# Audio tower on one core: expert pairs spread over row 7's attention, biases on VectorE, row 5's route earlier

## What is computed

```python
h = _L0_tok_ref(x, ...)      # per row: gelu(x W1 + b1), gelu(. W2 + b2), . W3 -> sigmoid -> lengths;
                             # Xnew = interp_weights(cumsum(lengths)) @ x      (750 -> 375 tokens)
h = h + _L0_attn_ref(_layernorm(h), ...)
                             # rmsnorm, qkv; softmax(q) over the 64 of a head, softmax(k) over tokens + 8 memory
                             # keys; context = k v^T; out = context q; @ w_out + b_out; rmsnorm
h = h + _L0_ffn_ref(_layernorm(h), ...)
# in _L0_ffn_ref, over all rows together:
routes = jnp.argmax(probs, axis=-1)
pos = jnp.take_along_axis(jnp.cumsum(oh, axis=0), routes[:, None], axis=1)[:, 0] - 1
y = jnp.einsum('ecd,efd->ecf', buf, expert_w) + expert_b[:, None, :]
out = jnp.where(keep[:, None], gathered, xf) * route_probs[:, None]
```

## Time and profile before

| what | value |
|---|---|
| median of 3 runs | 478.9 us (478.19 to 482.76) |
| the profiled execution, its own time | 480.63 us |
| its span in the trace | 478.8 us |
| mean granted TensorE clock in it | 0.953 |
| TensorE, VectorE, ScalarE, GpSimd busy | 421.4, 361.0, 190.6, 136.2 us |
| start of step 7's values of row 6, end of its layer 2 | 348.5, 362.4 us |
| the ending (after layer 2 of row 7) | 362.4 us to the end of the span |

### The profile page before, as it was taken

The page is one execution under the profiler, slowest core; times in us unless marked ns, Lnnn a source line. Parts: engine busy times, 40 slices in busy tenths (PEclk is TensorE's granted clock), DMA queues, the critical chain, the costliest instruction groups (busy, mean ns, idle before and its releaser), DMA issues.

```text
span 478.8 us, 7541 instructions
## 1 busy us (share of the span) xinstructions
PE 421.4 (88%) x2535; PEld 363.6 (76%) x2535; DVE 361.0 (75%) x946; ACT 190.6 (40%) x377; POOL 136.2 (28%) x189
## 2 busy tenths in 40 slices
PE   3976699999999999999999999999996869987790
PEld 2755587898889788978897988789886847776790
DVE  3543867896999799979988998899899456438761
ACT  2412414831582177128604841593154227520000
POOL 4200120013026313530451055007304410004682
PEclk9997899999999999999999999999999979998885
DMA  5674002000100100020002000200000361130133
GB/s 168 155 269 133 1 2 64 2 0 24 43 2 18 43 23 1 18 64 2 2 18 64 2 1 17 65 1 13 6 1 0 80 104 42 41 84 11 31 94 94
DMA packets 30795, 21.57 MB, mean 45 GB/s; under 512 B 4666, under 2 KB 28312, under 8 KB 30390
## 3 DMA queue, kind: packets, MB, share of 16 engines
q1 hardware_dynamic: 27862, 18.73, 13.8%
q0 software_dynamic: 2880, 2.35, 2.1%
q10 hardware_dynamic: 16, 0.02, 0.0%
HBM read 14.41 MB, written 6.62 MB: 44 GB/s over the span
## 4 chain that ended last, share of the span: by engine, by line
PE 59%; DVE 14%; issue 12%; SPq 5%; DMA 4%; POOL 3%; ACT 2%; POOLq 0%; ACTq 0%; DVEq 0%
PE psB L875 7%; PE psB L877 7%; PE psB L876 7%; PE psC L901 6%; PE psC L838 4%; PE psC L1002 4%; PE psC L839 4%; PE psC L840 4%; DMA xt<-in_x 3%; DVE qsum L1403 2%; POOL A L575 2%; PE psC L985 2%; SPq L407 2%; DVE rs L1362 2%; DVE h2b L1293 1%
## 5 line engine op out<-in xcount | busy, mean ns | idle before, releaser
L875 PE MATMUL psB<-W2h,h1l 128*125 128x512 f32 x192 | 79.0, 412 | 0.0
L877 PE MATMUL psB<-W2h,h1h 128*125 128x512 f32 x192 | 77.0, 401 | 0.0
L876 PE MATMUL psB<-W2l,h1h 128*125 128x512 f32 x192 | 76.8, 400 | 0.0
L619 ACT ACTIVATE h2b<-h2b 125x512 f32<-125x512 f32 x48 | 30.3, 631 | 99.7 <-DVE h2b L1286 99.6
L1286 DVE TENSOR_TENSOR h2b<-psB,b2r 125x512 f32<-125x512 f32 x48 | 33.0, 688 | 20.8 <-PE psB L877 20.3
L877 PEld LDWEIGHTS psB<-W2h,h1h 128*125 128x125 f32 x192 | 36.4, 190 | 9.1
L493 POOL TENSOR_TENSOR sg<-euler,sg 125x6 f32<-125x6 f32 x8 | 15.2, 1896 | 98.0 <-DVE sg L1300 98.0
L876 PEld LDWEIGHTS psB<-W2l,h1h 128*125 128x125 f32 x192 | 36.7, 191 | 7.9
L875 PEld LDWEIGHTS psB<-W2h,h1l 128*125 128x125 f32 x192 | 36.6, 191 | 8.0 <-DVE h1l L1277 0.2
L614 ACT ACTIVATE h<-psA,b1c 128x376 f32<-128x376 f32 x64 | 36.0, 580 | 15.2 <-PE psA L840 14.9
L1293 DVE CUSTOM_DVE_ANT_0 h2b<-h2b,W3r 125x512 f32<-125x512 f32 x48 | 32.3, 684 | 2.8 <-ACT h2b L619 2.7
(11 more groups left out here) (248 smaller groups left out, 1004.2 us busy)
## 6 DMA issues: line engine op xcount, KB each, us to landing
xt<-in_x SPq DMA_DIRECT2D x8, 375.0 KB
xs<-in_x SPq DMA_DIRECT2D x8, 312.5 KB
slot_x<-ebr SPq DMA_DIRECT2D x2, 960.0 KB, 9.2
basef<-in_L_tok_W SPq DMA_DIRECT2D x1, 1024.0 KB, 6.1
ebr<-in_L_ffn_expert_b SPq DMA_DIRECT2D x1, 1024.0 KB, 6.8
ewf<-slot_x SPq DMA_DIRECT2D x2, 480.0 KB, 6.3
h2b<-slot_x SPq DMA_DIRECT2D x2, 480.0 KB, 8.1
slot_y<-h SPq DMA_DIRECT2D x4, 240.0 KB, 2.5
```

The costliest lines, as they stand in the source:

```text
L619: nc.scalar.activation(slot, slot, ACT.Gelu).then_inc(c_g2.sem, 1)
L875: mm(ps, lo, W2h[:, k, :], start=k == 0, stop=False)
L876: mm(ps, hi, W2l[:, k, :], start=False, stop=False)
L877: last = mm(ps, hi, W2h[:, k, :], start=False, stop=k == HK - 1)
```

## The change

- Step 7 only: TensorE does row 5's `xf_transposed` between row 6's values and queries, its `logits` behind the queries and its `positions` behind group 4 of layer 2, and then row 6's keys. VectorE does `normal2`, `take_logits`, `route` and `place_in_expert` of row 5 between row 6's query maxima. Row 6's first keys wait for `place_in_expert` of row 5 (c_pp), and positions wait for c_xl instead of c_ke.
- The ending: the expert pairs begin right behind row 6's attend and stand between all of row 7's steps. Row 6's xf, logits and positions stand around row 7's attend.
- The bias matmul is gone. `expert_bias(p)` on VectorE adds the bias while it moves psB to ya and yb; ScalarE's `take_outputs` is gone, and one semaphore, s_eyb, takes the place of s_ya and s_yb.
- `take_m` of row 6 moves from VectorE to ScalarE (four scaled copies). Row 7's moments1 and normal1 go ahead of row 6's out_norm on VectorE; row 6's moments2 and normal2 come later.
- GpSimd does the scatter of row 5 ahead of row 7's sigmoid power, and the first three fetches around row 7's norm2 and norm3.
- The dense experts: 6, then 4 of row 6's, then row 7's 16, then row 6's last 6. Row 6's choice is spread in xn instead of osq. Rows finish in the order 0, 1, 7, 2, 6, 3, 4, 5.

The diff, cut to its core:

```diff
-        ROW_ORDER = [0, PRIOR, 1, 2, 3, LAST, 4, 5]
+        ROW_ORDER = [0, 1, LAST, 2, PRIOR, 3, 4, 5]
...
             def ending():
+                scatter(PRIOR - 1, PRIOR - 2)
                 sigmoid_pow(LAST, PRIOR)
-                scatter(PRIOR - 1, PRIOR - 2)
                 norm1(LAST, PRIOR)
                 norm2(PRIOR, PRIOR - 1)
                 norm3(PRIOR, PRIOR - 1)
                 counts(PRIOR, PRIOR - 1)
-                norm2(LAST, PRIOR)
-                norm3(LAST, PRIOR)
                 after(pool, c_idx, SLOT_ROWS - 1, 9)
                 pool.wait_ge(s_yst, 128)
                 fetch(0)
+                norm2(LAST, PRIOR)
+                fetch(1)
+                norm3(LAST, PRIOR)
+                fetch(2)
                 counts(LAST, PRIOR)
-                for b in range(1, SLOT_ROWS):
+                for b in range(3, SLOT_ROWS):
...
+            def take_m(b, prev):
+
+                after(act, c_m, b, 1)
+                after(act, c_rk, b, 1)
+                if prev is not None:
+                    after(act, c_fin, prev, 1)
+                for p in range(PAIRS):
+                    last = nc.scalar.activation(m[:, p, :], psC[1][:, p * C:(p + 1) * C], ACT.Copy, scale=rk[:, p:p + 1])
+                last.then_inc(c_ms.sem, 1)
...
+                if row_is(b, PRIOR) and p == 0:
+                    after(pe, c_pp, b - 1, 1)
...
-                if f is not None:
+                if row_is(f, PRIOR):
+                    after(pe, c_xl, f, 1)
+                elif f is not None:
                     after(pe, c_ke, f, 1)
...
             def expert_products(p):
                 pe.wait_ge(s_exc, p + 1)
-                if p == 0:
-                    pe.wait_ge(s_eb, 16)
                 if p < 2:
                     after(pe, c_b2, LAST, TJ)
                 else:
-                    pe.wait_ge(s_ya, p - 1)
-                    pe.wait_ge(s_yb, p - 1)
+                    pe.wait_ge(s_eyb, p - 1)
                 ps, xT = psB[p % 2], sxT[:, p % 2, :]
-                bias = ebr[0:1, 2 * p:2 * p + 2, :].rearrange("p e c -> p (e c)").unsqueeze(1).to_broadcast([1, 2, 2 * C])
-                mm(ps[0:TS, :].rearrange("p (t n) -> p t n", t=2), ones[0:1, 0:TS], bias, start=True, stop=False)
                 for i in range(2):
                     w = ewT[:, 2 * p + i, :]
...
                 last.then_inc(s_ey, 1)
...
                 if f is not None:
                     for j in range(GJ):
                         values(f, before(f), j)
+                if m == LAST:
+                    xf_transposed(k, m)
+                if f is not None:
                     for j in range(GJ):
                         queries(f, before(f), j)
+                if m == LAST:
+                    logits(k, m)
                 if m is not None:
                     layer2(m, before(m), 4)
-                if k is not None:
+                if m == LAST:
+                    positions(k, f)
+                if k is not None and m != LAST:
                     xf_transposed(k, m)
                 if f is not None:
                     keys(f, before(f), 0)
-                if k is not None:
+                if k is not None and m != LAST:
                     logits(k, m)
                 if f is not None:
                     for p in range(1, PAIRS):
...
                 if m is not None:
                     x_next(m, k)
                     layer2(m, before(m), 5)
-                if k is not None:
+                if k is not None and m != LAST:
                     positions(k, f)
...
                 warp(f, before(f))
                 fold(k, before(k))
                 attend(k, before(k))
+                expert_tokens(0)
                 xn_transposed(f, before(f))
+                expert_tokens(1)
+                expert_products(0)
                 for j in range(GJ):
                     values(f, before(f), j)
-                queries(f, before(f), 0)
-                expert_tokens(0)
-                queries(f, before(f), 1)
-                queries(f, before(f), 2)
+                expert_tokens(2)
+                for j in range(GJ):
+                    queries(f, before(f), j)
+                expert_products(1)
                 keys(f, before(f), 0)
-                expert_products(0)
-                expert_tokens(1)
+                expert_tokens(3)
+                expert_products(2)
                 keys(f, before(f), 1)
-                expert_products(1)
-                expert_tokens(2)
+                expert_tokens(4)
+                expert_products(3)
                 keys(f, before(f), 2)
+                expert_tokens(5)
+                expert_products(4)
                 keys(f, before(f), 3)
-                expert_products(2)
-                expert_tokens(3)
+                expert_tokens(6)
+                expert_products(5)
                 for j in range(KJ):
                     k_transposed(f, k, j)
-                expert_products(3)
-                expert_tokens(4)
+                expert_tokens(7)
+                expert_products(6)
+                context(f, k)
+                expert_products(7)
+                for j in range(GJ):
+                    q_transposed(f, k, j)
+                fold(f, k)
                 xf_transposed(k, None)
-                context(f, k)
-                expert_products(4)
-                expert_tokens(5)
+                attend(f, k)
                 logits(k, None)
-                for j in range(GJ):
-                    q_transposed(f, k, j)
-                expert_products(5)
-                expert_tokens(6)
-                fold(f, k)
                 positions(k, None)
-                expert_products(6)
-                expert_tokens(7)
-                expert_products(7)
-                attend(f, k)
                 chosen_on_rows(k)
                 dense_bias(k)
-                for e in range(9):
+                for e in range(6):
                     dense(k, e)
                 xf_transposed(f, None)
                 logits(f, None)
-                for e in range(9, E):
+                for e in range(6, 10):
                     dense(k, e)
                 chosen_on_rows(f)
                 positions(f, None)
                 dense_bias(f)
                 for e in range(E):
                     dense(f, e)
+                for e in range(10, E):
+                    dense(k, e)
...
+            def expert_bias(p):
+                if p == 0:
+                    dve.wait_ge(s_eb, 16)
+                    after(dve, c_h1l, LAST, 2)
+                    after(dve, c_warp, LAST, 1)
+                dve.wait_ge(s_ey, p + 1)
+                pair = slice(2 * p, 2 * p + 2)
+                ps = psB[p % 2][:].rearrange("p (e c) -> p e c", c=C)
+                vec.tensor_tensor(ya[:, pair, :], ps[0:TS, 0:2, :], ebr[0:TS, pair, :], ALU.add)
+                vec.tensor_tensor(yb[:, pair, :], ps[0:TS, 2:4, :], ebr[0:TS, pair, :], ALU.add).then_inc(s_eyb, 1)
...
+                if m == LAST:
+                    normal2(k, before(k))
                 if f is not None:
                     query_max(f, before(f), 0)
-                if k is not None:
+                if k is not None and m != LAST:
                     normal2(k, before(k))
+                if m == LAST:
+                    take_logits(k, before(k))
+                    route(k, before(k))
                 if f is not None:
                     query_max(f, before(f), 1)
                     query_max(f, before(f), 2)
+                if m == LAST:
+                    place_in_expert(k, before(k))
                 if m is not None:
...
-                take_m(k, r)
                 moments1(f, k)
+                normal1(f, k)
                 out_norm(k, r)
-                normal1(f, k)
+                xn_lo(f, k)
                 residual(k, r)
-                xn_lo(f, k)
-                moments2(k, r)
-                for j in range(GJ):
-                    query_max(f, k, j)
-                for p in range(PAIRS):
-                    key_max(f, k, p)
-                normal2(k, r)
                 keep_h(f, k)
+                expert_bias(0)
+                query_max(f, k, 0)
+                query_max(f, k, 1)
+                expert_bias(1)
+                query_max(f, k, 2)
+                expert_bias(2)
+                key_max(f, k, 0)
+                key_max(f, k, 1)
+                expert_bias(3)
+                key_max(f, k, 2)
+                key_max(f, k, 3)
+                expert_bias(4)
                 key_sum(f, k)
+                expert_bias(5)
                 query_sum(f, k)
                 query_norm(f, k)
+                expert_bias(6)
+                moments2(k, r)
+                expert_bias(7)
+                normal2(k, r)
+                take_m(f, k)
                 take_logits(k, r)
                 route(k, r)
                 spread_choice(k)
+                out_norm(f, k)
```

(32 more changed lines are left out.)

70 lines of the change are left out of this document (26 added, 44 removed).

## The result

The changed kernel takes 482.96 us (median of 9 runs), the kernel before 478.9. The ratio is 1.008, interval 1.0049 to 1.0111: 0.4 to 1.1% slower. The 0.8% lies within the 1% that I called no change, but it goes the other way than my forecast, and the time is 1 us above my range. The profiled execution took 482.93 us with a span of 481.1.

A forecast was written before the change was run, and what follows sets the result against it. TensorE was busiest, but row 7's chain through GpSimd's order set the end. 467.6 for the experts + 3.4 finishes + 3.8 store gave span 474.8, a 4.0 us gain; 475.0 us predicted, range 467.5 to 482.

The forecast's parts named there:

- Part 1: Step 7, row 5's route ahead of row 6's queries: layer 2's group 5 +6.3 us, row 6's attend +7.3 us.
- +7.3 for +7.95: Row 7's power starts 7.95 us later; VectorE used to take it 0.4 late, so row 6's attend moves 7.3.
- Parts 2 and 3: Biases to VectorE (8.4 us off TensorE) and pairs between row 7's steps: attend(7) carried at 420.4, 8.7 us early.
- Part 4: GpSimd's and VectorE's order behind attend(7): most gain given back, row 7's first token at 449.6, was 451.12.
- dense 9, chosen and positions 1.2: Behind row 7's logits, after route and four row 6 tokens: ninth expert, chosen and positions add 1.2 us.
- 8.7 us shrink to 1.5: Of attend(7)'s 8.7 us lead, 1.5 us is left at row 7's first token.
- Part 5: Last stretch: 22 experts end at 467.6, four finishes take 3.4, the store 3.8; span 474.8, a 4.0 us gain.
- then the store, 3.8: At the end: 3.8 us from the last finish to the end of the span, for the store.
- the upper half-rate choice: Last 22 experts: half rate for up to 6.9 us, upper end of 16.9 to 18.7 us.
- the detour's number (480.0): Rival: step 7's route costs over 6.3 us, with group 4, keys and group 5 at half; no difference, chance 0.16.
- The slow one: Rival: the last stretch's 22 experts stay at half rate, 487.2 us, chance 0.10.
- The quicker one: Rival: clock stays up after short gaps and the scatter is over in time; 6 us saved, 469.0, chance 0.24.

The follow-up runs named there:

- the fillers: Changed kernel plus 28, 8 and 9 matmuls nobody reads in TensorE's three idle stretches behind row 7's attend: 476.75 us, ratio 0.9958 to the kernel before.
- row 6's experts together: Changed kernel with rows 0 to 2 finished early and row 6's last six experts ahead of row 7's: 478.12 us, ratio 0.9975 to the kernel before.
- the repaired one: Changed kernel with step 7's old order, unread matmuls in TensorE's gaps and rows 0 to 2 finished early: 466.0 us, ratio 0.9727 to the kernel before.

## Why the prediction was wrong

I forecast a span of 474.8 and the like-for-like end is 483.25, 8.45 later. By the steps:

**Part 1's totals were right, the second in part by luck.** Layer 2 ends at 366.25, with 2.15 368.4 (368.7 forecast); attend(6) at 388.64, with 2.15 390.8 (391.0). Inside it errors cancel. The queries ran at full rate, but at half they would have cost only 0.3 to 0.4 us, as two other profiles show. The scatter took 7.9 us, not 9.8, so the power started 2.4 early, as soon as z was ready. Then 1.6 of it went: 0.35 in the two matmul groups ahead of `context`, 0.85 in `context` (5.40 against 4.55 before) and 0.45 in m (a wait of 1.23 for 0.78). And the 0.6 that I took off (+7.3 for +7.95) was not there. `context` is a half-rate stretch that I never priced: it stands behind a gap of 3.62 us, and row 7's takes 2.84 for the same matmuls; no run closes that gap. Undoing step 7 gave 6.4 us at the end, against the 7.3 that I priced it at.

**Parts 2 and 3 were right.** Attend(7) ends at 420.4 with the shift (420.4 forecast), values start at 393.3 (393.4). An addition takes 0.42 us (0.37 taken, 0.30 to 0.56 bounded), and the biases are worth all of their 8.4 us there.

**Part 4 failed at "dense 9, chosen and positions 1.2".** Up to row 6's own_experts all came within 0.5 us. Then experts 0 to 5 ran at half rate for nearly all of their time and ended at 441.9, 1.8 us above my middle and 0.9 above my upper bound. And behind row 7's logits I let experts 6 to 8 run beside VectorE's tokens and counted only the ninth; but they wait 2.72 us for the first token and then ran mostly at half: 7.7 us from logits to place instead of 5.0. With the fillers this takes 6.0 at full rate, so 1.0 of the 2.7 is the overlap that I had wrong and 1.7 the rate. I had applied the half rate after such a gap to the queries and the last stretch, not to experts 6 to 9. Row 7's first token is 4.3 us late, and "8.7 us shrink to 1.5" became a loss of 2.8.

**Part 5's term "then the store, 3.8" failed.** Before, stores were spread over 20 us, because finishes waited for gathers. The change lets four rows finish within 3.2 us, and each store takes some 1.8: the tail is 7.1, 3.3 more. I had priced a store alone and no queue ahead of it. The last stretch itself took 19.0 us for 18.0, the upper half-rate choice (which took 6.9 us of half rate from before, where the rows give 6.7). 4.3 + 1.0 + 3.3 - 0.2 (the finishes) = 8.4 of the 8.45.

Of the rivals, the detour's number (480.0) came nearest, still 3 us short and for the wrong reason: its keys and group 5 ran at full rate in the changed kernel, though the run with row 6's experts together shows that they can fall. The slow one didn't occur: in the last stretch the rate came back after some 6.5 us. The quicker one fell with the half rates. That a gap of 2.7 us is followed by half rate in one profile and not in another is shown, in the last stretch (ten of eleven) as at the queries (two of ten); what decides it stays open, and so does what shifts whole profiles by some us in steps 1 to 6.

## What to carry to other kernels

When the last wait is removed, price what it had spaced out: here stores of 192 KB that had been spread now queue, and finishing early rows in idle time gave 1.3%. A gap of over 2 us in front of a row of matmuls cost the gap and, in most profiles, 1.7 to 3.2 us more behind it, so count both for each gap of the new order, or close it. A step moved out of an engine's idle time (the norms behind gathers, the gathers behind norms) has to be weighed for whichever chain ends last in that version; much the same edit gave 3 us to the changed kernel and cost the repaired one 10.

## What was not expected of the hardware

GpSimd's scatter took 7.9 us in the changed kernel and 9.8 before. In between lies where VectorE's operations of 125x1536 fall: a multiplication of 125x3 took 0.19 to 0.20 us in the changed kernel and 1.82 us beside one of them, with step 7 undone:

```profile
367.47 1.82 POOL L541 TENSOR_TENSOR place<-place,keep 125x3 f32<-125x3 f32 x1
367.49 1.75 DVE L1405 SCALAR_TENSOR_TENSOR qa<-qa,rq 125x1536 f32<-125x1536 f32 x1
```

Two queues didn't speed up output stores that kept the DMA engines busy for only 0.35 of the time at 103 GB/s, while each store shows some five packets in flight. And TensorE's clock could fall in the midst of keys and layer 2 with no gap inside (0.72 in 360 to 366, row 6's experts together).
